# Layer norm's factors and its scale and shift on GpSimd, in a two-layer transformer kernel on one core

## The chip, the cores and the metric

The kernel runs on one NeuronCore of a Trainium2 chip. Five engines work side by side, each through its own instruction queue in program order, and meet at semaphores: TensorE (PE; its weight loads are shown as PEld), VectorE (DVE), ScalarE (ACT), GpSimd (POOL) and SyncE (SP), which here issues the DMAs. The metric is the device time of one execution in microseconds (us).

## The reference

Four residual blocks on x of 16 x 512 x 128 floats (16 batches, 512 tokens, 128 features), each behind a layer norm without learned weights:

```
def _layernorm(x, axis=-1, eps=1e-05):
    m = jnp.mean(x, axis=axis, keepdims=True)
    v = jnp.var(x, axis=axis, keepdims=True)
    return (x - m) / jnp.sqrt(v + eps)
...
x = x + attention0(_layernorm(x))   # 16 heads of 8 features, softmax, output projection and bias
x = x + gated_ffn(_layernorm(x))    # silu(x @ wg.T) * (x @ wu.T) @ wd.T, 384 hidden features
x = x + attention1(_layernorm(x))   # as layer 0, with an rms norm on q and k
x = x + lora_mix(_layernorm(x))     # base linear, plus 8 experts of rank 8 weighted by a softmax router
```

Everything on the way to the change is float32.

## The kernel before

A batch's 512 tokens lie as 4 tiles of 128 partitions. The work is written out by hand as a pipeline over batches of alternating slots, X i and Y i; slots X 2 to Y 13 are one hardware loop of 12 turns, the others are written out. A slot has 32 steps s, each with two half-steps h = 2s and 2s+1, and in a half-step every engine has its fixed share, in program order:

- TensorE: one score tile for the attention (`attend_score`, L1112, banks 0 to 2 of PSUM), one score tile for the running maximum of the next attention (`max_score`, L1102, banks 3 to 5), every fourth half-step the product with the values (`attend_pv`, L1127), and at set half-steps a "piece" of the dense work, all pieces through one PSUM bank (`gen`).
- ScalarE: one exponential for each half-step (`exp_unit`, L647), which frees the attention's bank, and copies of pieces out of PSUM.
- VectorE: one row maximum for each half-step (`max_tile`, L853), which frees the maximum's bank, and the small reductions.
- GpSimd: products that need only SBUF (L539 to L575).

Each of the two score streams has three banks, so TensorE can be three half-steps ahead of the exponential and three ahead of the maximum. Where the maximum's stream passes from one attention to the next (half-steps 38 and 39) the second tile of the new one waits for the last maximum of the old one, two half-steps back (`free_at`, L127).

There are four norms for each batch, told apart by k: norm 1 (before the feed-forward part), norm 2 (before attention 1), norm 3 (before the expert part) and norm 0, which normalises the batch two ahead, straight from `x_in`. Norms 1, 0 and 2 lie in a Y slot, norm 3 in an X slot. A norm goes through the engines like this. VectorE takes statistics (`stats`, L830, `bn`), folds them into mean and variance (`moments`, L838, `mv`) and begins the factors (`factors_in`, L844 and L845: `neg_mean` = -mean, `vpe` = variance + eps, four columns each). GpSimd takes `rstd` = vpe ** -0.5 (L532) and `shift` = neg_mean * rstd (L534). ScalarE applies them, one instruction for each of the four token tiles (`apply_norm`, L653: `xn` = x * rstd + shift). TensorE turns `xn` (`turn_norm`, L1078), and ScalarE copies the result to `xnt`. The places are: norm 1 moments and factors at h 21 of Y, applied at s 12, turned at h 27; norm 0 statistics at h 30 and 32, moments at h 34, factors at h 36, applied at s 21 and 22, turned at h 3 of the next X; norm 2 moments and factors at h 45, applied at s 24, turned at h 51; norm 3 moments at h 27, factors at h 28 of X, applied at s 17 and 18, turned at h 39.

Between norm 1 and norm 2 the feed-forward part runs: `w_gate` product, tanh (`th`, L697), `gs` on VectorE (L902), `w_up` product, `up`, `ht` = up * gs on GpSimd (`up_mul`, L568), three times. The `w_up` product writes the bank that `gs` reads, so it waits for `gs`. `parts_high` and `parts_low` (L859, L868) split finished maxima every sixteenth half-step.

At the start, slot Y -1 works alone: norm 0 of batches 0 and 1, the first projections, the weights.

## Time and profile before

| | |
|---|---|
| runs | 2129.20, 2131.88, 2137.05 us; median 2131.88 |
| profiled execution | 2135.92 us, its span 2134.1 us |
| PE busy | 1831.3 us (86%) |
| DVE busy | 1598.7 us (75%) |
| ACT busy | 1432.2 us (67%) |
| POOL busy | 432.8 us (20%) |

The busy time of an engine says how much lies in its queue, not whether others wait for it; of TensorE it is modelled. What decides are the waits: which instruction stood last before TensorE could go on. The rows for that are below, from slot Y 8 (1086.0 to 1151.0 us of the span), which is one turn of the loop like the others. In a timeline row the first number is the start, the second the time that the group took, and a bracket tells how long the engine stood idle before it and what released it; neighbouring instructions of one engine overlap by up to 0.1 us, so a duration is a little more than the place it takes in the queue.

### The profile page before, as it was taken

The page shows a single profiled execution, that of the slowest core. Times are in us where ns is not written, and L with a number is a line of the kernel's source. Part 1 is how long each engine was busy: PE and PEld are TensorE (multiplying, and loading weights), DVE is VectorE, ACT ScalarE, POOL GpSimd, SP SyncE. Part 2 cuts the span into 40 slices and gives each one's busy share as a digit, 9 for nine tenths or more (in the row PEclk, how much of TensorE's full clock was granted, in tenths as well). Part 3 has the DMA queues.
Part 4 walks back from the last instruction along what each step waited for, and adds up shares of the span by engine and source line. Part 5 has one row for each costly group of instructions (what it writes and reads, how often), then busy time and mean ns, then how long its engine had stood idle before and what let it go on. Part 6 is the DMA issues. An engine that isn't in the chain of part 4 may idle for free.

```text
span 2134.1 us, 38850 instructions
## 1 busy us (share of the span) xinstructions
PE 1831.3 (86%) x10958; PEld 688.9 (32%) x10958; DVE 1598.7 (75%) x3593; ACT 1432.2 (67%) x2921; POOL 432.8 (20%) x570
## 2 busy tenths in 40 slices
PE   4858989888988988888898888989898998998775
PEld 1232323333332333333333333323333332333322
DVE  4538888887878778778787878777787878888471
ACT  2716686776767677677766767676776768776543
POOL 2112131221212122121212212120121213121200
PEclk9957999999999999999999999999999999999867
DMA  5203223050413205041320504123050413212020
GB/s 109 71 11 101 47 67 96 18 140 17 118 34 96 65 17 140 17 115 37 81 81 17 140 17 115 36 71 91 17 140 17 115 37 79 79 35 59 29 53 16
DMA packets 162647, 140.87 MB, mean 66 GB/s; under 512 B 38761, under 2 KB 144050, under 8 KB 162482
## 3 DMA queue, kind: packets, MB, share of 16 engines
q1 hardware_dynamic: 162482, 139.29, 24.7%
q14 instruction: 137, 1.12, 0.2%
q8 instruction: 28, 0.46, 0.1%
HBM read 77.38 MB, written 55.57 MB: 62 GB/s over the span
## 4 chain that ended last, share of the span: by engine, by line
PE 37%; issue 24%; DMA 11%; ACT 9%; POOL 8%; DVE 8%; SPq 3%; ACTq 0%; POOLq 0%; DVEq 0%
PE ps L1127 11%; PE ps L1112 7%; PE ps L1148 5%; ACT probs L647 5%; DVE neg_max L853 4%; PE ps L1102 4%; DMA k_stack<-k_rows 4%; DMA rden_all<-rden_rows 3%; PE ps L1078 3%; PE ps L1153 2%; PE ps L1191 2%; DMA k_rows<-kp 2%; PE ps L1141 2%; POOL o_raw L551 2%; POOL qk L561 2%
## 5 line engine op out<-in xcount | busy, mean ns | idle before, releaser
L853 DVE TENSOR_REDUCE neg_max<-ps 128x1 f32<-128x512 f32 x2048 | 1316.4, 680 | 196.8 <-PE ps L1102 167.7
L647 ACT ACTIVATE probs<-ps 128x512 f32<-128x512 f32 x2048 | 1093.4, 599 | 324.5 <-PE ps L1112 309.0
L1102 PE MATMUL ps<-k_stack,q_stack 48*128 48x512 bf16 x2048 | 702.5, 402 | 86.6 <-DVE neg_max L853 46.4
L1112 PE MATMUL ps<-q_stack,k_stack 50*128 50x512 bf16 x2048 | 655.1, 391 | 79.8 <-ACT probs L647 75.7
L1127 PE MATMUL ps<-probs,v_aug 128*32 128x512 f32 x4096 | 568.1, 628 | 1.0
L1112 PEld LDWEIGHTS ps<-q_stack,k_stack 50*128 50x128 bf16 x2048 | 150.8, 95 | 525.1 <-ACT probs L647 342.4
L1102 PEld LDWEIGHTS ps<-k_stack,q_stack 48*128 48x128 bf16 x2048 | 159.3, 94 | 280.3 <-DVE neg_max L853 239.4
L551 POOL TENSOR_TENSOR o_raw<-o_raw,rden_all 128x512 f32<-128x512 f32 x64 | 81.3, 1270 | 569.6 <-DMA rden_all<-rden_rows 569.6
L1127 PEld LDWEIGHTS ps<-probs,v_aug 128*32 128x32 f32 x4096 | 81.7, 109 | 136.3 <-issue 81.5
L1153 PE MATMUL ps<-wo,o_raw 128*128 128x128 f32 x512 | 81.8, 326 | 43.2 <-POOL o_raw L551 43.1
L653 ACT ACTIVATE xn<-x,shift,rstd 128x128 f32<-128x128 f32 x192 | 80.5, 484 | 52.4 <-POOL shift L534 52.4
L568 POOL TENSOR_TENSOR ht<-up,gs 128x512 f32<-128x512 f32 x48 | 60.9, 1269 | 248.6 <-ACT up L628 248.6
L561 POOL TENSOR_TENSOR qk<-qk,nw_y 128x128 f32<-128x128 f32 x128 | 47.3, 407 | 304.8 <-DVE nw_y L940 304.8
L532 POOL TENSOR_TENSOR rstd<-vpe,half_neg 128x4 f32<-128x4 f32 x64 | 64.5, 1008 | 211.6 <-DVE vpe L845 211.6
L890 DVE TENSOR_TENSOR x<-ps,res 128x512 f32<-128x512 f32 x32 | 22.1, 691 | 105.4 <-PE ps L1153 105.4
L1153 PEld LDWEIGHTS ps<-wo,o_raw 128*128 128x128 f32 x512 | 75.1, 233 | 69.7 <-issue 42.8
L628 ACT ACTIVATE xnt<-ps 128x512 f32<-128x512 f32 x64 | 38.0, 593 | 79.0 <-PE ps L1078 78.6
L1078 PE MATMUL ps<-ident,xn 128*128 128x128 f32 x256 | 57.3, 364 | 31.8 <-ACT xn L653 31.8
L890 DVE TENSOR_TENSOR x<-ps,x 128x512 f32<-128x512 f32 x32 | 22.1, 691 | 83.0 <-PE ps L1191 49.0
L628 ACT ACTIVATE up<-ps 128x512 f32<-128x512 f32 x48 | 28.7, 597 | 63.3 <-PE ps L1148 63.3
L1078 PEld LDWEIGHTS ps<-ident,xn 128*128 128x128 f32 x256 | 36.8, 180 | 97.8 <-issue 97.8
L1148 PE MATMUL ps<-xnt,w_gate 128*128 128x256 f32 x192 | 58.2, 428 | 8.9 <-ACT xnt L628 3.2
(103 smaller groups left out, 1499.4 us busy)
## 6 DMA issues: line engine op xcount, KB each, us to landing
q_stack<-q_rows SPq DMA_DIRECT2D x128, 192.0 KB, 3.7
k_stack<-k_rows SPq DMA_DIRECT2D x128, 192.0 KB, 4.6
rden_all<-rden_rows SPq DMA_DIRECT2D x64, 256.0 KB
q_rows<-qp SPq DMA_DIRECT2D x32, 384.0 KB, 2.6
k_rows<-kp SPq DMA_DIRECT2D x32, 384.0 KB, 2.9
q_rows<-qp SPq DMA_DIRECT2D x32, 256.0 KB, 3.0
k_rows<-kp SPq DMA_DIRECT2D x32, 256.0 KB, 3.0
x_in<-in_L_attn_x SPq DMA_DIRECT2D x16, 256.0 KB, 2.8
```

What stands on the lines that cost most here:

```text
L551: pool.tensor_tensor(o_raw[l][:, c, :], o_raw[l][:, c, :], rden_all[l][:, c, :], ALU.mult).then_inc(att_ready[l], 1)
L561: last = pool.tensor_tensor(x[:, t, :, :], x[:, t, :, :], wide(inv[:, t, :, None], 2, HD), ALU.mult)
L628: return act.activation(dst, src, ACT.Copy)
L647: act.activation(probs[:, u % RING, :], ps[:, bank_of(l, u), :], ACT.Exp).then_inc(exps, 1)
L653: last = act.activation(xn[k][:, t, :], x[:, t, :], ACT.Identity, bias=shift[k][:, t:t + 1], scale=rstd[k][:, t:t + 1])
L853: dve.tensor_reduce(neg_max[l][:, pair // 2, col:col + 1], ps[:, BANKS + bank_of(l, n), :], AX.X, ALU.max, negate=True).then_inc(max_taken, 1)
L1078: return pe.transpose(dst, src, ident[0:n, 0:n])
L1102: pe.matmul(ps[:, BANKS + bank_of(l, m), :], q_stack[l][row:row + KROWS, pair, tok:tok + 128], k_stack[l][row:row + KROWS, pair, :], start ...
L1112: pe.matmul(ps[:, bank_of(l, u), :], k_stack[l][row:row + AROWS, pair, tok:tok + 128], q_stack[l][row:row + AROWS, pair, :], start=True, s ...
L1127: last = pe.matmul(acc[32 * j:32 * j + 32, :], v_aug[l][:, kt, 8 * e + 2 * group + pp, :], probs[:, (u + j) % RING, :], start=(s == 0 and ...
L1148: return pe.matmul(gen[:, 256 * half:256 * half + 256], w, xt[:, 256 * half:256 * half + 256], start=True, stop=True)
L1153: last = pe.matmul(gen4[:, t, :], o_raw[l][:, c, 128 * t:128 * t + 128], wo[l][:, c, :], start=c == 0, stop=c == 1)
```

## The change

`neg_mean` and `factors_in` go. GpSimd computes `vpe` itself and the shift from the mean with its sign kept, and it applies the norm, four instructions of 128 x 128 with two operands read per partition (x * rstd - shift). ScalarE's `apply_norm` goes, with all its calls.

```diff
             def norm_factors(k, b):
+                wait_apart(pool, mv_done[k], b + 1, passed)
+                pool.tensor_scalar(vpe[k][:, :], mv[k][:, :, 1], LN_EPS, None, ALU.add).then_inc(var_ready[k], 1)
                 pool.wait_ge(var_ready[k], b + 1)
                 pool.tensor_tensor(rstd[k][:, :], vpe[k][:, :], half_neg[:, :], ALU.pow).then_inc(rstd_ready[k], 1)
                 pool.wait_ge(rstd_ready[k], b + 1)
-                pool.tensor_tensor(shift[k][:, :], neg_mean[k][:, :], rstd[k][:, :], ALU.mult).then_inc(shift_ready[k], 1)
+                pool.tensor_tensor(shift[k][:, :], mv[k][:, :, 0], rstd[k][:, :], ALU.mult).then_inc(shift_ready[k], 1)
+            def apply_norm(k, x, b):
+                if k in (0, 3):
+                    need(pool, read[f"xt{k}"], b)
+                elif k == 1:
+                    need(pool, read["xt2"], b)
+                else:
+                    pool.wait_ge(read["xt1"], b + 1)
+                wait_apart(pool, shift_ready[k], b + 1, passed)
+                for t in range(TT):
+                    last = pool.tensor_scalar(xn[k][:, t, :], x[:, t, :], rstd[k][:, t:t + 1], shift[k][:, t:t + 1],
+                                              ALU.mult, ALU.subtract)
+                last.then_inc(xn_ready[k], 1)
...
                     if "M1" in have:
                         normalise(0, 1, i)
                         norm_factors(1, i)
+                        apply_norm(1, x1, i)
                         for c in range(NH):
                             up_mul(c, i)
                     if "S0" in have and at >= 0:
                         norm_factors(0, i + 2)
+                        apply_norm(0, x_in, i + 2)
                     if "M1" in have:
                         norm_factors(2, i)
+                        apply_norm(2, x2, i)
...
-            def apply_norm(k, x, tiles, b):
-                act.wait_ge(shift_ready[k], b + 1)
-                for t in tiles:
-                    last = act.activation(xn[k][:, t, :], x[:, t, :], ACT.Identity, bias=shift[k][:, t:t + 1],
-                                          scale=rstd[k][:, t:t + 1])
-                if tiles[-1] == TT - 1:
-                    last.then_inc(xn_ready[k], 1)
...
-            def factors_in(k, b):
-                dve.wait_ge(mv_done[k], b + 1)
-                dve.tensor_scalar(neg_mean[k][:, :], mv[k][:, :, 0], -1.0, None, ALU.mult)
-                dve.tensor_scalar(vpe[k][:, :], mv[k][:, :, 1], LN_EPS, None, ALU.add).then_inc(var_ready[k], 1)
```

VectorE's order around norm 0 in a Y slot (`gs` is the feed-forward gate, `ht` is on GpSimd). Before:

```order
L838 BN_AGGR mv<-bn 128x2 x4
L853 TENSOR_REDUCE neg_max<-ps 128x1 x2
L844 TENSOR_SCALAR neg_mean<-mv 128x4
L845 TENSOR_SCALAR vpe<-mv 128x4
L853 TENSOR_REDUCE neg_max<-ps 128x1
L859 CAST neg_high<-neg_max 128x16
L902 SCALAR_TENSOR_TENSOR gs<-th,ps 128x512
```

Now:

```order
L840 BN_AGGR mv<-bn 128x2 x4
L848 TENSOR_REDUCE neg_max<-ps 128x1 x3
L854 CAST neg_high<-neg_max 128x16
L897 SCALAR_TENSOR_TENSOR gs<-th,ps 128x512
```

The two small instructions between the second and the third row maximum are gone; nothing else on VectorE moved.

GpSimd's order through norms 1, 0 and 2 of a Y slot. Before:

```order
L532 TENSOR_TENSOR rstd<-vpe,half_neg 128x4
L534 TENSOR_TENSOR shift<-neg_mean,rstd 128x4
L568 TENSOR_TENSOR ht<-up,gs 128x512 x3
L532 TENSOR_TENSOR rstd<-vpe,half_neg 128x4
L534 TENSOR_TENSOR shift<-neg_mean,rstd 128x4
L532 TENSOR_TENSOR rstd<-vpe,half_neg 128x4
L534 TENSOR_TENSOR shift<-neg_mean,rstd 128x4
```

Now:

```order
L531 TENSOR_SCALAR vpe<-mv 128x4
L533 TENSOR_TENSOR rstd<-vpe,half_neg 128x4
L535 TENSOR_TENSOR shift<-mv,rstd 128x4
L547 TENSOR_SCALAR xn<-x,rstd,shift 128x128 x4
L583 TENSOR_TENSOR ht<-up,gs 128x512 x3
L531 TENSOR_SCALAR vpe<-mv 128x4
L533 TENSOR_TENSOR rstd<-vpe,half_neg 128x4
L535 TENSOR_TENSOR shift<-mv,rstd 128x4
L547 TENSOR_SCALAR xn<-x_in,rstd,shift 128x128 x4
L531 TENSOR_SCALAR vpe<-mv 128x4
L533 TENSOR_TENSOR rstd<-vpe,half_neg 128x4
L535 TENSOR_TENSOR shift<-mv,rstd 128x4
```

Behind each shift stand the four instructions that apply the norm, and ahead of each power stands `vpe`; the order of the norms and of `ht` is as it was.

ScalarE's order at the very start (the table load belongs to the first activation). Before:

```order
L653 ACT_TABLE_LOAD
L653 ACTIVATE xn<-x_in,shift,rstd 128x128 x4
L628 ACTIVATE xnt<-ps 128x512
```

Now:

```order
L649 ACT_TABLE_LOAD
L649 ACTIVATE xnt<-ps 128x512
```

The table load, which waited for the shift, now stands behind the wait for the turned tile.

## Rows read from the trace of the kernel before

**Rows 1.** Slots X 8 and X 9: busy us (instructions) of PE, PEld, DVE, ACT, POOL; clock; DMA.
```profile
1027.60:1086.00 58.40, 51.29 (x336) 19.09 (x336) 47.14 (x106) 44.33 (x91) 15.53 (x23) 0.97 0.42 111
...
1151.00:1211.90 60.90, 53.77 (x336) 19.66 (x336) 47.10 (x106) 44.37 (x90) 15.53 (x23) 0.92 0.38 106
```
**Rows 2.** Timeline of VectorE around norm 1 in slot Y 8.
```profile
1107.48 0.38 DVE L838 BATCH_NORM_AGGREGATE mv<-bn 128x2 f32<-128x6 f32 x4
1107.90 0.17 DVE L844 TENSOR_SCALAR neg_mean<-mv 128x4 f32<-128x4 f32 x1
...
1108.05 0.69 DVE L853 TENSOR_REDUCE neg_max<-ps 128x1 f32<-128x512 f32 x1
1108.65 0.17 DVE L868 TENSOR_TENSOR neg_max<-neg_max,neg_high 128x16 f32<-128x16 f32 x1
```
**Rows 3.** Timeline of GpSimd, the same norm.
```profile
1108.22 1.01 POOL L532 TENSOR_TENSOR rstd<-vpe,half_neg 128x4 f32<-128x4 f32 x1 [7.39 <-DVE vpe L845]
1109.30 0.20 POOL L534 TENSOR_TENSOR shift<-neg_mean,rstd 128x4 f32<-128x4 f32 x1
```
**Rows 4.** Timeline of ScalarE, the same norm.
```profile
1109.60 1.63 ACT L653 ACTIVATE xn<-x,shift,rstd 128x128 f32<-128x128 f32 x4
```
**Rows 5.** Timeline of TensorE, the same norm.
```profile
1108.79 0.39 PE L1102 MATMUL ps<-k_stack,q_stack 48*128 48x512 bf16 x1 [0.81 <-DVE neg_max L853]
...
1110.38 1.06 PE L1127 MATMUL ps<-probs,v_aug 128*32 128x512 f32 x8
1111.38 0.66 PE L1078 MATMUL ps<-ident,xn 128*128 128x128 f32 x4
```
**Rows 6.** Timeline of VectorE around norm 0's factors in slot Y 8.
```profile
1121.32 0.69 DVE L853 TENSOR_REDUCE neg_max<-ps 128x1 f32<-128x512 f32 x1 [0.17 <-PE ps L1102]
1121.92 1.07 DVE L844 TENSOR_SCALAR neg_mean<-mv 128x4 f32<-128x4 f32 x1
...
1122.98 0.68 DVE L853 TENSOR_REDUCE neg_max<-ps 128x1 f32<-128x512 f32 x1
1123.69 0.18 DVE L859 CAST neg_high<-neg_max 128x16 bf16<-128x16 f32 x1
1123.87 0.69 DVE L902 SCALAR_TENSOR_TENSOR gs<-th,ps 128x512 f32<-128x512 f32 x1
```
**Rows 7.** Timeline of GpSimd at the same place.
```profile
1121.70 1.26 POOL L568 TENSOR_TENSOR ht<-up,gs 128x512 f32<-128x512 f32 x1 [3.15 <-ACT up L628]
```
**Rows 8.** Timeline of ScalarE at the same place.
```profile
1122.89 0.63 ACT L697 ACTIVATE th<-ps 128x512 f32<-128x512 f32 x1
```
**Rows 9.** Timeline of TensorE at the same place.
```profile
1122.91 0.38 PE L1112 MATMUL ps<-q_stack,k_stack 50*128 50x512 bf16 x1
1123.71 0.39 PE L1102 MATMUL ps<-k_stack,q_stack 48*128 48x512 bf16 x1 [0.43 <-DVE neg_max L853]
1124.03 1.06 PE L1127 MATMUL ps<-probs,v_aug 128*32 128x512 f32 x8
1125.03 1.13 PE L1148 MATMUL ps<-xnt,w_up 128*128 128x256 f32 x4
```
**Rows 10.** Group of all `neg_mean`: busy us, mean ns, idle before.
```profile
L844 DVE TENSOR_SCALAR neg_mean<-mv 128x4 f32<-128x4 f32 x64 | 22.4, 350 | 1.3
```
**Rows 11.** Norm 2 of slot Y 8, timeline of ScalarE.
```profile
1136.40 1.65 ACT L653 ACTIVATE xn<-x,shift,rstd 128x128 f32<-128x128 f32 x4 [0.37 <-POOL shift L534]
```
**Rows 12.** Norm 2 of slot Y 8, timeline of TensorE.
```profile
1138.36 0.66 PE L1078 MATMUL ps<-ident,xn 128*128 128x128 f32 x4
```
**Rows 13.** TensorE in slot X 8, behind the application of norm 3.
```profile
1064.03 0.50 PE L1102 MATMUL ps<-k_stack,q_stack 48*128 48x512 bf16 x2 [1.72 <-DMA k_stack<-k_rows]
```
**Rows 14.** GpSimd's nearest instruction in size, timeline of slot X 8.
```profile
1039.45 2.96 POOL L561 TENSOR_TENSOR qk<-qk,nw_y 128x128 f32<-128x128 f32 x8 [20.31 <-DVE nw_y L940]
```
**Rows 15.** Timeline of ScalarE at the start.
```profile
7.04 1.28 ACT L653 ACT_TABLE_LOAD   x1 [7.04 <-POOL shift L534]
17.30 1.65 ACT L653 ACTIVATE xn<-x_in,shift,rstd 128x128 f32<-128x128 f32 x4 [8.97 <-DVE bq_scaled L983]
```

More of the change, by code:

```diff
@@ L202, in build @@
         rstd = [sb(f"rstd{k}", [128, TT]) for k in range(4)]
-        neg_mean = [sb(f"neg_mean{k}", [128, TT]) for k in range(4)]
         shift = [sb(f"shift{k}", [128, TT]) for k in range(4)]
@@ L598, in slot @@
                         norm_factors(3, i - 2)
+                        apply_norm(3, x3, i - 2)
                         mix(i - 2)
@@ L604, in slot @@
                         norm_factors(0, 0)
+                        apply_norm(0, x_in, 0)
                         for n in (0, 1):
@@ L609, in slot @@
                         norm_factors(0, 1)
+                        apply_norm(0, x_in, 1)
                     if "M1" in have:
@@ L721, in slot @@
                     act.wait_ge(bq_ready, 1)
-                    apply_norm(0, x_in, range(TT), 0)
                     take("xt0", xnt[0][:, :], 0)
@@ L728, in slot @@
                     weights_out()
-                    apply_norm(0, x_in, range(TT), 1)
                     take_max(0, 0, 0)
@@ L764, in slot @@
                         if "E" in have:
-                            if s in (17, 18):
-                                apply_norm(3, x3, (2 * s - 34, 2 * s - 33), i - 2)
                             if s == 19:
@@ L773, in slot @@
                     else:
-                        if "S0" in have and s in (21, 22):
-                            apply_norm(0, x_in, (2 * s - 42, 2 * s - 41), i + 2)
                         if "M1" in have:
-                            if s == 12:
-                                apply_norm(1, x1, range(TT), i)
                             if s == 13:
@@ L784, in slot @@
                                 take_up((s - 15) // 2, i)
-                            if s == 24:
-                                apply_norm(2, x2, range(TT), i)
                             if s == 25:
@@ L980, in slot @@
                     moments(0, 0)
-                    factors_in(0, 0)
                     dve.wait_ge(first_loaded, 16 * 6)
@@ L990, in slot @@
                     moments(0, 1)
-                    factors_in(0, 1)
                 for h in range(2 * STEPS):
@@ L1019, in slot @@
                                 moments(3, i - 2)
-                            if h == 28:
-                                factors_in(3, i - 2)
                             if h in (43, 44, 45):
@@ L1035, in slot @@
                                 moments(0, i + 2)
-                            if h == 36:
-                                factors_in(0, i + 2)
                         if "V0" in have and h in (16, 17):
@@ L1051, in slot @@
                                 moments(1, i)
-                                factors_in(1, i)
                             if at == 0 and h == 23:
@@ L1063, in slot @@
                                 moments(2, i)
-                                factors_in(2, i)
                             if h in (53, 55):
```

## The prediction

> **What bounds the kernel now.** I read the busy times first, then the waits, then timelines of one turn of the loop around each norm. No engine is full: in slot X 8, of 58.40 us, TensorE is busy 51.29, VectorE 47.14, ScalarE 44.33, GpSimd 15.53 [rows 1]. TensorE goes in program order through both score streams and stops where either ring of three banks is not free, so what counts at each norm is which engine frees the bank that TensorE asks for next. At norm 1 that is VectorE: TensorE idled 0.81 us for a row maximum just after the moments [rows 5], and VectorE goes through its maxima there without a gap. At norm 0's factors it is VectorE again (0.43 us idle, and a start 0.80 us after the score tile ahead of it, 1123.71 against 1122.91) [rows 9]. Behind norm 3 it is neither: TensorE waits 1.72 us for a DMA that fills the next key stack [rows 13].
>
> ScalarE's part is 4 instructions in 1.63 us at norm 1 [rows 4]. The exponentials behind them are late by that, but TensorE is meanwhile in the value product (1110.38 to 1111.38) and then in the turn (1111.38 on) [rows 5]; it asks for none of these exponentials before it is through. So the time that ScalarE loses is mostly not on the path, and the 16 x 4 x 1.65 = 106 us that it gets back are no term of my sum.
>
> **The two instructions that go from VectorE.** Without a neighbour on GpSimd they are short: the moments end at 1107.48 + 0.38 = 1107.86, the next maximum starts at 1108.05 [rows 2], so they take 0.19 us of VectorE's queue.
>
> At norm 0 it is another thing: `neg_mean`, four columns, takes 1.07 us [rows 6]. It starts at 1121.92, while GpSimd's `ht` runs from 1121.70 to 1122.96, and ends just behind it [rows 7]. In all, `neg_mean` is busy 22.4 us [rows 10]; 64 at 0.17 make 10.9, and the other 11.5 at 0.90 each make 13 such cases: norm 0 of batches 3 to 15, one in each turn in which `ht` runs beside it. The Trainium skill (SBUF — State Buffer, "Who interferes with whom") has this as an exclusive lock that VectorE's two-port or two-input instructions share with GpSimd; the trace agrees.
>
> What is the stall worth? Without the two instructions the maximum at 1122.98 starts at 1121.92, 1.06 earlier. The score tile that waits for it (1123.71) can follow its predecessor at 1122.91, 0.80 earlier, so the value product goes from 1124.03 to 1123.23 and the `w_up` product from 1125.03 to 1124.23 [rows 9]. But that product also needs `gs`, and `gs` needs the tanh, which ends at 1122.89 + 0.63 = 1123.52 [rows 8]; `gs` then runs from 1123.55 for 0.69 and frees the bank about 0.05 later, at 1124.29. `gs` is what is late next, and the place gives 1125.03 - 1124.30 = 0.73 us. The cast (L859), in front of `gs`, would wait for `ht` in its turn, until 1122.96, which is 0.4 us before `gs` can start: covered by the tanh. Behind that TensorE and ScalarE take turns on the feed-forward's pieces, all of which move together. **13 x 0.73 = 9.5 us.**
>
> **The chain from moments to the turn.** Now, at norm 1: moments end 1107.86, power 1108.22 to 1109.23, shift 1109.30 to 1109.50, application 1109.60 to 1111.23, turn 1111.38 [rows 2 to 5]: 3.52 us. TensorE comes out of a value product 1.00 us after its start (1124.03 to 1125.03 in [rows 9]), here at 1110.38 + 1.00 = 1111.38 too: chain and queue end together.
>
> After: a handover (0.09, as `vpe` ended 1108.13 and the power began 1108.22), `vpe` on GpSimd (0.20, the price of its shift, four columns too), handover 0.08, power 1.01, handover 0.08, shift 0.20, handover 0.08, three starts and one full application, 0.14 to TensorE. That is 1.88 + 3t + d, with t from start to start of an application and d the length of the last. No row shows the application's form on GpSimd (128 columns, one tensor, two scalars per partition). Its bound from below is the 0.20 of the shift [rows 3]; the nearest row is `scale_qk`, two tensors of 128 columns: 8 in 2.96 us, that is a start every t = 0.36 and d = 0.41 for one alone [rows 14]; from above it is the power's 1.01 [rows 3]. I take the nearest, since it has the same columns: 1.88 + 1.09 + 0.41 = 3.38 us, 0.14 less than now.
>
> The Trainium skill (GPSIMD Engine Reference, 3.1) gives one-input bodies 1.03 cycles for each element and two-input ones about 2.6; an estimate by it is 128 x 1.03 / 1.2 GHz = 0.11 us and the fixed 0.2, some 0.3 us an instruction in place of 0.36 to 0.41. By that the chain is 0.3 us shorter still, and norm 1's gain below goes from 0.14 to its limit of 0.19, 0.8 us in all.
>
> At norm 1 VectorE's 0.19 brings TensorE to the turn 3.33 us after the moments, xn comes at 3.38: the gain is 0.14. **16 x 0.14 = 2.2 us.** At norm 2, application ends 1138.05 [rows 11], turn 1138.36 [rows 12]; the chain is 0.17 us ahead of TensorE, which comes through VectorE's maxima as before. Both gain, so VectorE's 0.19 counts in full. **16 x 0.19 = 3.0 us.** At norm 3 what VectorE gives up is swallowed by the 1.72 us of DMA wait [rows 13], whose chain began earlier: 0. Norm 0's application is turned a slot later: 0. GpSimd's longer queue (0.2 + 1.5 us for each norm) delays nobody at these places: it stood idle 7.39 us ahead of norm 1's power [rows 3], and 3.15 us ahead of the second `ht` [rows 7].
>
> **The start.** Now ScalarE waits until 17.30 (a late load of the first projections' biases), applies for 1.65, and TensorE follows 0.14 later; the table load was over by then [rows 15]. After, GpSimd has xn long before, and TensorE turns as soon as the loads are in; but the table load (1.28) now stands behind the wait for that turn. Gain 1.65 + 0.14 - 1.28 = **0.5 us**; the first slots and the last norm have the bare chain, 3 x 0.14 = **0.4 us**.
>
> Sum: 9.5 + 2.2 + 3.0 + 0.5 + 0.4 = 15.6 us. Against the profiled execution that is 2135.9 - 15.6 = 2120.3 us; the median of the runs lies 4.0 below that execution: **2116.3 us**, 0.73% faster. A difference under 0.5% (10.7 us) is about what a measurement of this kernel can't tell from none.
>
> **The clock.** X 8 took 58.40 us at a granted clock of 0.97, X 9 60.90 at 0.92, with the same work [rows 1]. So the dips to the lower level (1.2 in place of 2.4 GHz), which come in short stretches behind pauses of TensorE, move single slots by up to 2.5 us. 0.8 us of pause goes in each turn, others shift; I put +-7 us on the sum for it and leave the middle.
>
> **Rivals.** (a) GpSimd's application is slow. The chain is 1.88 + 4t + 0.05 and each 0.1 us on t costs 0.4 us at 32 turns. It eats the other 10 us when 16(1.93 + 4t - 3.52) + 16(1.93 + 4t - 3.64) = 10, at t = 0.49, and makes the kernel slower by over 0.5% from t = 0.58. For it: two scalars are read per partition, which no GpSimd row has, and the power takes 1.01 us for four columns. At t = 0.75 it is 43 - 10 = +33 us: 2165 us. Against it: it is a plain multiply and subtract with one tensor. Chance 0.16, of which 0.04 ends within 0.5%.
>
> (b) The lock moves. GpSimd is busy 1.7 us longer for each norm; a VectorE instruction that needs the shared pair and comes in that stretch waits, by up to 0.9 us as above. Perfetto Trace Analysis of the Trainium skill ("Optimizing Scalar/DVE Operations") says for this that offloading between the two might not help. Behind norm 1 stands L868, which reads two SBUF tensors; it took 0.17 us at 1108.65 while the power ran [rows 2, 3], and is over before the application; at the others I find maxima out of PSUM. If one instruction a turn loses 0.7 us all the same, 16 x 0.7 = 11 us go back: 2127 us. The same time comes if the 0.73 is absorbed by the next wait. Chance 0.20.
>
> (c) ScalarE's relief pays. If TensorE did lack the late exponentials, norms 1 and 2 would give half of 1.63 us more each: 32 x 0.8 = 26 us, 2090 us. [rows 4, 5] speak against it. Chance 0.12.
>
> My forecast has 0.52; within it the clock leaves about 0.09 inside 0.5%. **Faster by over 0.5%: 0.43 + 0.12 = 0.55; within: 0.09 + 0.20 + 0.04 = 0.33; slower: 0.12.** Range: the forecast with the clock and t from 0.25 to 0.45 spans 2107 to 2128, (b) takes it to 2134; to leave no more than 0.2 out I reach some way to (c) and (a): 2100 to 2138 us.
>
> **What would show it.** No VectorE instruction of about 1 us beside `ht`; `w_up` of the third gate 0.7 us sooner behind its tanh; GpSimd's four applications in 1.5 us; moments to turn 3.4 us at norm 1 and TensorE waiting for xn by 0.05 us; ScalarE's busy time 106 us less with more idle time in front of its exponentials; the same DMA wait behind norm 3. I am wrong if t is over 0.45, if L859 or L868 stretch, or if slots X shrink as much as slots Y.

## The result, and the profile after

The changed kernel takes 2238.68 us (median of 4 runs, 2232.58 to 2243.99), the kernel before 2132.68 us beside it: a ratio of 1.0495, 95% interval 1.0461 to 1.0529. It is 4.95% slower, 106 us; the forecast was 2116.3 us with 2138 as its upper end. The profiled execution of the changed kernel has a span of 2242.2 us, that of before 2134.1.

First the page of the changed kernel: ScalarE's busy time fell from 1432.2 us to 1339.5, by 93 us (the forecast had 106), and GpSimd's rose from 432.8 to 650.4, by 218 us.

```profile
PE 1885.5 (84%) x10958; PEld 693.6 (31%) x10958; DVE 1583.6 (71%) x3465; ACT 1339.5 (60%) x2665; POOL 650.4 (29%) x890
...
PEclk8858999899898988999899899988999999998867
```

The groups of GpSimd's new instructions, in the view by line (busy us, mean ns of one, idle time before it): the applications, 192 for norms 1 to 3 and 64 for norm 0, then the power, `vpe` and the shift, which cost about what was supposed.

```profile
L547 POOL TENSOR_SCALAR xn<-x,rstd,shift 128x128 f32<-128x128 f32 x192 | 150.4, 796 | 9.6 <-issue 7.2 <-POOL shift L535 2.2
L547 POOL TENSOR_SCALAR xn<-x_in,rstd,shift 128x128 f32<-128x128 f32 x64 | 50.0, 795 | 3.0 <-issue 2.4 <-POOL shift L535 0.5
L533 POOL TENSOR_TENSOR rstd<-vpe,half_neg 128x4 f32<-128x4 f32 x64 | 66.4, 1037 | 5.3
L531 POOL TENSOR_SCALAR vpe<-mv 128x4 f32<-128x4 f32 x64 | 15.0, 234 | 142.3 <-DVE mv L840 142.1
L535 POOL TENSOR_TENSOR shift<-mv,rstd 128x4 f32<-128x4 f32 x64 | 12.9, 202 | 5.0
```

An application takes 0.80 us. The same norm 1 of slot Y 8 as in [rows 2 to 5], now in the timelines of VectorE, GpSimd and TensorE:

```profile
1161.58 0.38 DVE L840 BATCH_NORM_AGGREGATE mv<-bn 128x2 f32<-128x6 f32 x4
1161.88 0.66 DVE L848 TENSOR_REDUCE neg_max<-ps 128x1 f32<-128x512 f32 x1
```

```profile
1162.16 0.23 POOL L531 TENSOR_SCALAR vpe<-mv 128x4 f32<-128x4 f32 x1 [5.61 <-DVE mv L840]
1162.48 1.04 POOL L533 TENSOR_TENSOR rstd<-vpe,half_neg 128x4 f32<-128x4 f32 x1
1163.60 0.20 POOL L535 TENSOR_TENSOR shift<-mv,rstd 128x4 f32<-128x4 f32 x1
1164.00 3.13 POOL L547 TENSOR_SCALAR xn<-x,rstd,shift 128x128 f32<-128x128 f32 x4 [0.20 <-issue]
```

```profile
1162.60 0.39 PE L1089 MATMUL ps<-k_stack,q_stack 48*128 48x512 bf16 x1 [0.51 <-DVE neg_max L848]
...
1164.19 1.07 PE L1114 MATMUL ps<-probs,v_aug 128*32 128x512 f32 x8
1167.27 0.75 PE L1065 MATMUL ps<-ident,xn 128*128 128x128 f32 x4 [2.01 <-POOL xn L547]
```

The moments end at 1161.58 + 0.38 = 1161.96, xn is there at 1164.00 + 3.13 = 1167.13, the turn starts at 1167.27: 5.31 us behind the moments where it was 3.52. Four applications in 3.13 us, 0.80 for the last, are a start every (3.13 - 0.80) / 3 = 0.78 us. TensorE is through with its value product at 1165.26 and stands for 2.01 us. Norm 2 is the same, with a turn at 5.30 us behind the moments where it was 3.64:

```profile
1196.41 0.63 PE L1065 MATMUL ps<-ident,xn 128*128 128x128 f32 x4 [1.88 <-POOL xn L547]
```

After the change both numbers are the same in nearly every turn of the loop. Before, norm 1 had 3.52 in most turns and up to 4.3 in some, and norm 2 had 4.5 or 4.6 in five.

TensorE's waits for xn in all (us, times, longest), after:

```profile
PE ps L1065 <- POOL xn L547: 76.0, 33, 7.3
```

Before, it waited at 5 places, the longest of them 19.1 us at the start:

```profile
PE ps L1078 <- ACT xn L653: 31.8, 5, 19.1
```

At the place of [rows 6 to 9], in the next stretch of slot Y 8, now ScalarE and TensorE, and VectorE beside GpSimd's `ht`:

```profile
1180.00 0.63 ACT L709 ACTIVATE th<-ps 128x512 f32<-128x512 f32 x1
```

```profile
1181.41 0.48 PE L1135 MATMUL ps<-xnt,w_up 128*128 128x256 f32 x1
```

```profile
1178.43 1.29 DVE L848 TENSOR_REDUCE neg_max<-ps 128x1 f32<-128x512 f32 x2 [0.17 <-PE ps L1089]
1179.76 0.37 DVE L854 CAST neg_high<-neg_max 128x16 bf16<-128x16 f32 x1
1180.67 0.69 DVE L897 SCALAR_TENSOR_TENSOR gs<-th,ps 128x512 f32<-128x512 f32 x1 [0.54 <-ACT th L709]
```

```profile
1178.83 1.27 POOL L583 TENSOR_TENSOR ht<-up,gs 128x512 f32<-128x512 f32 x1 [3.14 <-ACT up L649]
```

No instruction of 1.07 us is left here; the cast waits for the end of `ht` (0.37 us, it was 0.18) and is over 0.5 us before the tanh ends. The `w_up` product starts 1181.41 - 1180.63 = 0.78 us behind the tanh, where it was 1125.03 - 1123.52 = 1.51: the 0.73 us of the forecast, to the hundredth. It is so in every turn: at the third gate the distance was 1.51 at 13 places and 0.78 at 3, and is 0.77 or 0.78 at all 16.

A third thing changed, TensorE's clock. In the stretch from 300 to 1900 us the granted clock was 0.96 before and is 0.92 after (the second row below is after's, the first before's; behind the times come the busy times of PE, PEld, DVE, ACT and POOL, then the clock):

```profile
300.00:1900.00 1600.00, 1428.64 (x8831) 534.79 (x8828) 1278.93 (x2869) 1147.10 (x2346) 343.44 (x445) 0.96 0.26 70
```

```profile
300.00:1900.00 1600.00, 1400.06 (x8406) 513.31 (x8398) 1208.28 (x2645) 1026.65 (x2045) 501.88 (x684) 0.92 0.25 67
1080.00:1141.80 61.80, 54.31 (x340) 19.76 (x339) 47.93 (x106) 43.09 (x87) 18.96 (x28) 0.92 0.41 104
1209.30:1274.70 65.40, 58.13 (x339) 20.54 (x338) 48.08 (x106) 43.08 (x86) 18.95 (x28) 0.84 0.38 99
```

The last two rows are the changed kernel's slots X 8 and X 9, with the same work. The records of the clock in these traces have two values, full and half, so a granted clock of 0.92 is (1 - 0.92) x 2 x 61.80 = 9.9 us at the lower, and 0.84 is 20.9 us: 11.0 us more at the lower clock made the slot 3.6 us longer, **about 0.33 us for each us**. The line through X 3 to X 13 of this kernel, length against time at the lower clock, has a slope of 0.34. In all runs the mean clock was 0.930 for before (65 runs beside the experiments) and 0.899 for after (4): 299 and 452 us at the lower level.

Where the added stretches begin can be seen in the trace. In the two rows below the first is the norm 1 above up to the turn, the second the 3.4 us behind the wait for xn:

```profile
1160.00:1167.60 7.60, 5.07 (x30) 1.42 (x30) 5.58 (x18) 3.59 (x8) 4.60 (x7) 1.00 0.12 36
1167.60:1171.00 3.40, 3.40 (x13) 1.44 (x13) 1.29 (x2) 1.68 (x3) 0.00 (x0) 0.51 0.00 0
```

From 300 to 1900 us the changed kernel waits 24 times for 1.9 to 2.0 us for xn, and at 19 of these places a stretch at the lower clock begins, from 0.4 us ahead of the wait's end to 2.1 us behind it. They are 19 of its 45 such stretches and 68 us of its 249 at the lower clock. Before had 126 us there, in 32 stretches, and no wait for xn of this length. Another 72 us, in 10 stretches, begin behind the wait for the DMA of the key stack in slot X, where before had 17 us in 5; why these grew the traces don't show.

### The profile page after: what moved, and what is told of

Read it like the earlier page. It is cut to its first block and busy times, and to the rows that moved or that the text cites. A ratio compares the mean times of both kernels' runs of the same rounds, so it can differ in the third digit from the quotient of the medians.

```text
span 2242.2 us, 38884 instructions
## 1 busy us (share of the span) xinstructions
PE 1885.5 (84%) x10958; PEld 693.6 (31%) x10958; DVE 1583.6 (71%) x3465; ACT 1339.5 (60%) x2665; POOL 650.4 (29%) x890
## 5 line engine op out<-in xcount | busy, mean ns | idle before, releaser
L1089 PE MATMUL ps<-k_stack,q_stack 48*128 48x512 bf16 x2048 | 727.0, 418 | 91.7 <-DVE neg_max L848 46.5
L1099 PE MATMUL ps<-q_stack,k_stack 50*128 50x512 bf16 x2048 | 683.1, 408 | 64.9 <-ACT probs L668 60.5
L1114 PE MATMUL ps<-probs,v_aug 128*32 128x512 f32 x4096 | 586.4, 647 | 0.9
L566 POOL TENSOR_TENSOR o_raw<-o_raw,rden_all 128x512 f32<-128x512 f32 x64 | 81.2, 1268 | 517.3 <-DMA rden_all<-rden_rows 517.3
L547 POOL TENSOR_SCALAR xn<-x,rstd,shift 128x128 f32<-128x128 f32 x192 | 150.4, 796 | 9.6 <-issue 7.2
L1140 PE MATMUL ps<-wo,o_raw 128*128 128x128 f32 x512 | 71.9, 299 | 46.5 <-POOL o_raw L566 46.5
L1140 PEld LDWEIGHTS ps<-wo,o_raw 128*128 128x128 f32 x512 | 65.6, 208 | 73.0 <-issue 44.6
L1135 PE MATMUL ps<-xnt,w_gate 128*128 128x256 f32 x192 | 69.2, 495 | 7.5 <-ACT xnt L649 1.5
L590 POOL TENSOR_TENSOR coef<-gating,rm 128x64 f32<-128x64 bf16 x64 | 16.7, 292 | 197.1 <-DVE gating L963 197.1
L897 DVE SCALAR_TENSOR_TENSOR gs<-th,ps 128x512 f32<-128x512 f32 x48 | 33.0, 688 | 57.1 <-ACT th L709 57.1
```

The lines of the kernel that those rows point to most:

```text
L547: last = pool.tensor_scalar(xn[k][:, t, :], x[:, t, :], rstd[k][:, t:t + 1], shift[k][:, t:t + 1], ALU.mult, ALU.subtract)
L566: pool.tensor_tensor(o_raw[l][:, c, :], o_raw[l][:, c, :], rden_all[l][:, c, :], ALU.mult).then_inc(att_ready[l], 1)
L1089: pe.matmul(ps[:, BANKS + bank_of(l, m), :], q_stack[l][row:row + KROWS, pair, tok:tok + 128], k_stack[l][row:row + KROWS, pair, :], start ...
L1099: pe.matmul(ps[:, bank_of(l, u), :], k_stack[l][row:row + AROWS, pair, tok:tok + 128], q_stack[l][row:row + AROWS, pair, :], start=True, s ...
L1114: last = pe.matmul(acc[32 * j:32 * j + 32, :], v_aug[l][:, kt, 8 * e + 2 * group + pp, :], probs[:, (u + j) % RING, :], start=(s == 0 and ...
L1135: return pe.matmul(gen[:, 256 * half:256 * half + 256], w, xt[:, 256 * half:256 * half + 256], start=True, stop=True)
```

## The experiments

Each kernel's change against before is given by its ratio x 2136 us. "Chain" is the time from the end of the moments to the turn at norm 1 and norm 2, read in slot Y 8 as above.

**1. The application alone.** Before, with the four applications on GpSimd; the factors stay begun on VectorE. Since VectorE still negates the mean, the shift is added.

```diff
+            def apply_norm(k, x, b):
+...
+                    last = pool.tensor_scalar(xn[k][:, t, :], x[:, t, :], rstd[k][:, t:t + 1], shift[k][:, t:t + 1],
+                                              ALU.mult, ALU.add)
```

> The kernel before with the application alone moved to GpSimd; VectorE still begins the factors. Theory A (GpSimd's application takes 0.78 us from start to start, the chain from moments to turn grows from 3.5 to about 5.1 us at norms 1 and 2, and TensorE's longer pauses there bring more stretches at the lower clock): about +100 us, 2225 to 2245, granted clock near 0.90, neg_mean still 1.07 us at norm 0. Rival B (the loss comes from the factors on GpSimd, or from GpSimd and VectorE together): well under +60 us.

2130.59 us, ratio 0.9979 (0.9949 to 1.001): the time is where rival B had it, and theory A, which I held for nearly certain, that this half carries the slowness, missed by about 95 us. It fell with this row, the group of the applications:

```profile
L545 POOL TENSOR_SCALAR xn<-x,rstd,shift 128x128 f32<-128x128 f32 x192 | 83.8, 453 | 9.3 <-issue 7.2 <-POOL shift L534 1.9
```

0.453 us and not 0.796, a start every 0.43 us; chain 3.74 and 3.74 us. The same engine, shape and operands; the only thing that differs is the second operation, add in place of subtract. ScalarE is relieved of as much as in the changed kernel (1338.0 us busy), and nothing comes of it: rival (c) is out.

**2. The factors alone.** Before, with `vpe` and `neg_mean` computed on GpSimd; ScalarE applies.

```diff
+                wait_apart(pool, mv_done[k], b + 1, passed)
+                pool.tensor_scalar(vpe[k][:, :], mv[k][:, :, 1], LN_EPS, None, ALU.add)
+                pool.tensor_scalar(neg_mean[k][:, :], mv[k][:, :, 0], -1.0, None, ALU.mult).then_inc(var_ready[k], 1)
```

> The kernel before with the factors alone moved to GpSimd (one more small instruction there, the negated mean); ScalarE applies. Theory A: the 1.07 us of VectorE beside ht goes (about -9 us), the chain grows by 0.2 to 0.3 us at norms 1 and 2 (about +8 us): 2124 to 2138, clock 0.93. Rival B: clearly slower than before, 2170 or more.

2131.83 us, ratio 0.9977 (0.9946 to 1.0007). Chain 3.98 and 3.95 us, since a second short instruction stands ahead of the power; what the stall gives back goes into that. The time is in theory A's range for this half, and rival B, that the factors carry the loss, is out. So neither half, as these two kernels have it, makes the kernel slow; but the first had an add where the changed kernel has a subtract.

**3. Work in TensorE's wait.** The changed kernel, with 8 matmuls of zeros (bf16, 512 columns) ahead of the wait for xn at norms 1 and 2.

```diff
+                if k in (1, 2):
+                    fill(FILL)
                 pe.wait_ge(xn_ready[k], b + 1)
```

> The changed kernel with 8 matmuls of zeros (bf16, 512 columns, some 1.7 us at the full clock) on TensorE ahead of its wait for xn at norms 1 and 2, into the PSUM bank that the turn then overwrites. The wait is the same length, TensorE is busy in it. Theory A (half of the loss is the clock that falls behind the pause): 2175 to 2195 us, granted clock back to 0.93 or more, chain still 5.3 us. Rival C (all of the loss is waits; the clock's dips cost little): 2235 or more, since work is only added.

2209.1 us, ratio 1.0339 (1.0305 to 1.0373): between the two. The mean clock came back to 0.930 with a chain of 5.22 and 5.21 us, but the run has a cost of its own. In the waits of TensorE (us in total, times, longest) and in the DMA queues of this kernel:

```profile
PE ps L1102 <- issue: 59.5, 22, 3.3
...
q8 instruction: 128, 2.10, 0.4%
```

59.5 us in which TensorE waited for nothing that the profile shows, at 22 places at the loop's turn, and 128 packets of instructions in place of 28. I read this as TensorE fetching instructions anew in each turn of the longer program. The Trainium skill (Runtime: NRT & Kernel Launch, "Instruction fetch mechanics") has a stall of this kind for a taken branch whose target is not in the fetched window; the trace agrees, with 2.7 us each.

**4. Norm 0's factors early.** Before, with the two VectorE instructions of norm 0 issued right behind its moments, ahead of `ht`, and nothing else.

```diff
                                 moments(0, i + 2)
-                            if h == 36:
                                 factors_in(0, i + 2)
```

> The kernel before with norm 0's two factor instructions put right behind its moments (half-step 34 instead of 36), ahead of GpSimd's ht. Theory A of the stall (0.73 us a turn is on TensorE's path): neg_mean 0.17 us everywhere, 2118 to 2127 us. Rival D (what follows absorbs it): 2130 to 2134.

2124.74 us, ratio 0.9932 (0.9909 to 0.9955), 14.5 us faster. The group of `neg_mean`, 22.4 us in [rows 10]:

```profile
L844 DVE TENSOR_SCALAR neg_mean<-mv 128x4 f32<-128x4 f32 x64 | 10.7, 167 | 1.7
```

The distance from tanh to `w_up` is 0.78 us at all 16 places here too. **The stall's term of my sum (9.5 us) is confirmed by itself**, if anything too small (the interval is 9.6 to 19.4 us), and its cure needs two lines moved, and no other engine.

**5. One word.** The changed kernel with add in place of subtract. It computes something else (the mean is added and not taken away); the work is the same.

```diff
-                                              ALU.mult, ALU.subtract)
+                                              ALU.mult, ALU.add)
```

> The changed kernel with one word altered: the second operation of the application on GpSimd is an add in place of the subtract. What it computes is changed by that, the mean is added and not taken away; the work is otherwise the same. Theory (the subtract is what costs): an application starts every 0.43 us as in the run with the application alone, in place of 0.78, the chain from moments to turn at norm 1 is 2.04 + 3 x 0.43 + 0.45 + 0.14 = 3.9 us; against before that is +0.4 us at 16 turns of norm 1 and +0.25 at 16 of norm 2, and -9.5 (the stall beside ht) -6 (two short instructions gone from VectorE): 2125 to 2134 us. Rival (the move as a whole costs, by GpSimd's queue or by VectorE's casts beside it, and the word does little): 2200 us or more, with an application every 0.78 us still, or every 0.43 and the time kept.

2127.18 us, ratio 0.9941 (0.9912 to 0.9971), by the ratios 118 us below the changed kernel. The group of the applications, and GpSimd at norm 1 of slot Y 8:

```profile
L547 POOL TENSOR_SCALAR xn<-x,rstd,shift 128x128 f32<-128x128 f32 x192 | 83.3, 448 | 9.6 <-issue 7.2 <-POOL shift L535 2.2
...
1097.87 1.74 POOL L547 TENSOR_SCALAR xn<-x,rstd,shift 128x128 f32<-128x128 f32 x4 [0.20 <-issue]
```

Chain 3.92 and 3.91 us. VectorE is as busy as in the changed kernel (1582.7 us against 1583.6). **The whole loss hangs on the subtract.**

**6. Prices of forms.** Before, with instructions on tiles of their own at GpSimd's start.

```diff
+            pool.tensor_scalar(f1[:, 0:128], t_in[:, 0:128], t_s[:, 0:1], t_s[:, 1:2], ALU.mult, ALU.subtract)
+...
```

> Before, with some 35 instructions on tiles of their own put into GpSimd's start, to price forms of 128 and 512 float32 columns. Theory A (subtract itself is slow on GpSimd when its operand is a per-partition value): mult+add with two per-partition operands 0.43 us, mult+subtract 0.78, subtract alone with one such operand slower than mult alone by 0.35, subtract of two tensors as mult of two tensors (0.36). Theory B (only mult+add is a fused case and every other pair runs in two passes): subtract+mult and add+mult 0.78 too, and subtract alone as mult alone. With 512 columns the gap is 4 times as wide if it is a cost for each element, and the same 0.35 if it is a fixed one. The time of the whole is a few us over before.

One execution, 2143.07 us, made for its rows and not for its time. One row of each form from GpSimd's timeline. In this order: multiply and add; multiply and subtract; subtract and multiply; add and multiply; the first two with 512 columns (L557, L558); one scalar per partition, multiply (L559) and subtract (L562); two constants, multiply and add (L566), multiply and subtract (L569); two tensors, subtract (L572) and multiply (L575).

```profile
2.62 0.44 POOL L546 TENSOR_SCALAR f<-t_in,t_s 128x128 f32<-128x128 f32 x1
4.25 0.79 POOL L549 TENSOR_SCALAR f<-t_in,t_s 128x128 f32<-128x128 f32 x1
6.59 0.79 POOL L552 TENSOR_SCALAR f<-t_in,t_s 128x128 f32<-128x128 f32 x1
8.57 0.45 POOL L555 TENSOR_SCALAR f<-t_in,t_s 128x128 f32<-128x128 f32 x1
9.42 0.77 POOL L557 TENSOR_SCALAR f<-t_in,t_s 128x512 f32<-128x512 f32 x1
10.17 2.08 POOL L558 TENSOR_SCALAR f<-t_in,t_s 128x512 f32<-128x512 f32 x1
12.23 0.60 POOL L559 TENSOR_SCALAR f<-t_in,t_s 128x128 f32<-128x128 f32 x1
13.97 0.61 POOL L562 TENSOR_SCALAR f<-t_in,t_s 128x128 f32<-128x128 f32 x1
15.97 0.30 POOL L566 TENSOR_SCALAR f<-t_in 128x128 f32<-128x128 f32 x1
17.12 0.64 POOL L569 TENSOR_SCALAR f<-t_in 128x128 f32<-128x128 f32 x1
18.75 0.45 POOL L572 TENSOR_TENSOR f<-t_in 128x128 f32<-128x128 f32 x1
19.98 0.45 POOL L575 TENSOR_TENSOR f<-t_in 128x128 f32<-128x128 f32 x1
```

With two operations a subtract makes the instruction 0.35 us longer, in either place and with constants too (0.30 against 0.64). It is a price for each column: from 128 to 512 columns multiply and add grow by 0.33 us, 0.86 ns a column, multiply and subtract by 1.29 us, 3.36 ns a column. Two tensors cost 0.45 whether subtracted or multiplied, and with one operation and one scalar subtract and multiply are alike. So theory A was half right (it expected the single subtract to be slow) and theory B fell (add and multiply is as fast as multiply and add). A single operation with a scalar per partition takes 0.60, more than the two operations multiply and add; I can't say why.

**7. Two fillers in place of eight.** As 3, with two float32 matmuls, to keep the program short.

```diff
+                if k in (1, 2):
+                    pe.matmul(gen, filler[:, 0:128], filler[:, :], start=True, stop=True)
+                    pe.matmul(gen[:, 0:256], filler[:, 0:128], filler[:, 0:256], start=True, stop=True)
```

> The changed kernel with two float32 matmuls of zeros (512 and 256 columns, about 1.5 us together) on TensorE ahead of its wait for xn at norms 1 and 2; they are two instructions in place of the eight of the run before, so that TensorE's instruction stream is hardly longer. Theory (the long wait costs twice: 1.7 us direct at each of 32 turns, about 55 us, and the stretches at the lower clock behind it, the rest of the +106 with the stall's 9.5 and VectorE's 6 given back: about 60): no instruction waits of 2.6 us at the loop back, low stretches back to about the 126 us of before in the loop, and 2242 - 60 = 2165 to 2190 us. Rival (the clock is a bystander and the direct wait makes all of it): 2230 us or more with the clock at 0.93.

2185.33 us, ratio 1.0225 (1.0178 to 1.0271). The time is in the range expected, one sign is not: the fetch is there again, once a turn and longer.

```profile
PE ps L1101 <- issue: 47.9, 11, 4.6
...
1177.97 0.60 PE L1101 MATMUL ps<-q_stack,k_stack 50*128 50x512 bf16 x1 [4.44 <-issue]
```

Still the chain is as long as in the changed kernel (5.22 and 5.21 us), instruction fetches of 47.9 us come on top, and by the ratios it is 58 us faster than the changed kernel, with a mean clock of 0.938 against 0.899. So the rival is out (the direct wait does not make all of it), and the busy waits are worth at least these 58 us (45 to 70 by the two intervals). How much the clock makes can't be read from this run, since part of the fetch's 47.9 us is hidden.

**8. The application shared.** As 2, and at norms 1 and 2 ScalarE applies tiles 0 and 1, GpSimd tiles 2 and 3, with multiply and add.

```diff
+            def apply_half(k, x, b):
+...
+                for t in (2, 3):
+                    last = pool.tensor_scalar(xn[k][:, t, :], x[:, t, :], rstd[k][:, t:t + 1], shift[k][:, t:t + 1],
+                                              ALU.mult, ALU.add)
+...
-                                apply_norm(1, x1, range(TT), i)
+                                apply_norm(1, x1, (0, 1), i)
```

> Before, with both factors computed by GpSimd (as in the run of factors alone), and the application of norms 1 and 2 shared: ScalarE tiles 0 and 1, GpSimd tiles 2 and 3 with mult and add and the negated shift. Norms 0 and 3 are applied by ScalarE. Theory (my sum holds once the chain is no longer than before): chain 2.3 to the shift's end + 0.1 + 2 x 0.43 + 0.14 = 3.35 us, so 9.5 us for the stall and 16 x 2 x 0.17 = 5.5 for VectorE's queue come through: 2132 - 15 = 2117, 2112 to 2122 us. Rival (what VectorE gives up at norms 1 and 2 is not on the path): as the early norm 0, 2122 to 2127. Rival (the shared application costs in another way, xn in two halves or GpSimd beside VectorE's casts): 2130 or more.

**2102.92 us, ratio 0.9852 (0.9805 to 0.9899): the fastest kernel of the study**, 31.6 us below before, twice what its terms gave and outside of every range expected. The chain is 3.40 and 3.37 us. Norm 1 in slot Y 8, GpSimd, ScalarE, TensorE:

```profile
1091.35 0.89 POOL L546 TENSOR_SCALAR xn<-x,rstd,shift 128x128 f32<-128x128 f32 x2 [0.21 <-issue]
```

```profile
1091.18 0.88 ACT L669 ACTIVATE xn<-x,shift,rstd 128x128 f32<-128x128 f32 x2 [0.65 <-POOL shift L537]
```

```profile
1092.39 0.63 PE L1079 MATMUL ps<-ident,xn 128*128 128x128 f32 x4
```

**9. The same move with the right form.** All on GpSimd as in the change, but as (x + negated mean) x rstd, without a shift.

```diff
+                pool.tensor_scalar(shift[k][:, :], mv[k][:, :, 0], -1.0, None, ALU.mult).then_inc(var_ready[k], 1)
...
+                    last = pool.tensor_scalar(xn[k][:, t, :], x[:, t, :], shift[k][:, t:t + 1], rstd[k][:, t:t + 1],
+                                              ALU.add, ALU.mult)
```

> The changed kernel's move, all of it on GpSimd and with the right result, but written as (x + the negated mean) x rstd: add, then multiply. GpSimd computes vpe and the negated mean, then the power; there is no shift. Theory (the subtract alone made the change slow): 0.43 us from start to start, chain 0.20 + 0.25 + 0.1 + 1.01 + 0.2 + 3 x 0.43 + 0.45 + 0.14 = 3.65 to 3.95 us, as the run with the add in place of the subtract: 2118 to 2132 us. Rival (with the right values, or with the add first, it is slow): 2200 us or more.

2123.3 us, ratio 0.9949 (0.9922 to 0.9977), chain 3.97 and 3.96 us. What the change does, written so, is 0.5% faster than before; it is no better than moving two lines (4).

**10. Norm 0 early, and the application shared.** VectorE keeps its two instructions at norms 1 and 2.

```diff
                                 moments(0, i + 2)
-                            if h == 36:
                                 factors_in(0, i + 2)
...
                         norm_factors(1, i)
+                        apply_half(1, x1, i)
...
-                                apply_norm(1, x1, range(TT), i)
+                                apply_norm(1, x1, (0, 1), i)
```

> Before, with norm 0's factors begun on VectorE right behind its moments (as in the run of that alone) and the application of norms 1 and 2 shared between ScalarE (tiles 0, 1) and GpSimd (tiles 2, 3, multiply and add). VectorE keeps both of its short instructions. It asks what made the shared kernel 31 us faster where its terms gave 15. Theory A (what VectorE gives up at norms 1 and 2, 0.30 us each, is on the path once the chain is short): here TensorE comes out of its value product 3.5 us behind the moments as before, the chain of 2.7 us is ahead of it and gives nothing: 2118 to 2126 us, as with norm 0's factors early alone. Theory B (slack in the chain spares pauses and with them stretches of the lower clock): fewer of them, 15 to 20 in the loop in place of 30, and 2100 to 2112 us.

2125.12 us, ratio 0.9946 (0.9921 to 0.997): theory A. GpSimd's half of the application ends early, and the turn stands where it stood:

```profile
1109.33 0.88 POOL L543 TENSOR_SCALAR xn<-x,rstd,shift 128x128 f32<-128x128 f32 x2 [0.20 <-issue]
```

```profile
1110.01 1.06 PE L1139 MATMUL ps<-probs,v_aug 128*32 128x512 f32 x8
1111.00 0.66 PE L1090 MATMUL ps<-ident,xn 128*128 128x128 f32 x4
```

xn is ready at 1110.21, and TensorE turns at 1111.00, 3.52 us behind the moments as before, since it comes out of its value product only then. A shorter chain is worth nothing without VectorE's 0.3 us, and those are worth nothing without a short chain (2). Only both together (8) gain.

**11 and 12. One norm slow.** Kernel 9, with the changed kernel's own lines (subtract, 0.78 us a tile) for norm 1 alone, and for norm 2 alone.

```diff
-                        norm_factors(1, i)
-                        apply_norm(1, x1, i)
+                        norm_factors_sub(1, i)
+                        apply_norm_sub(1, x1, i)
```

> The kernel with add and multiply on GpSimd for norms 0, 2 and 3, and the changed kernel's own lines (multiply and subtract, 0.78 us a tile) for norm 1 alone: half of the slow applications on the path. The chain at norm 1 is 1.4 us longer than with the add. Theory (each long wait costs twice, direct and by the clock behind it): 16 x 1.4 = 22 us direct and about as much by lower clock, 2160 to 2185 us. Rival (the clock's share came from both waits lying in one slot, or from norm 3): the direct part alone, 2140 to 2150 us.

2169.85 us, ratio 1.017 (1.0132 to 1.0208).

> The counterpart of the run before: add and multiply for norms 0, 1 and 3, the changed kernel's own lines (0.78 us a tile) for norm 2 alone. Direct cost over the kernel with add and multiply everywhere: 16 x 1.4 = 22 us. With norm 1 slow the profile showed no more time at the lower clock than with none slow (113 us in the loop), with both slow 249. Theory P (it is the wait at norm 2, the last before slot X, that brings the lower clock): over 200 us low in the loop and 2175 to 2195 us. Theory C (only both together do, since the second long wait comes when the first has hardly been made good): about 110 to 150 us low and 2150 to 2170 us.

2183.78 us, ratio 1.0241 (1.018 to 1.0302). Over kernel 9 the one costs 47 us, the other 62 (to within 10 and 14 us), together 109; the changed kernel lies 117 above kernel 9 (1.0495 - 0.9949). So the times add up, and theory C, that only both together bring the loss, is out. Theory P was right in time and only partly in its sign: from 300 to 1900 us the profiled run has 184 us at the lower clock, not over 200. The same stretch has 113 us in kernel 9, 113 with norm 1 slow and 249 in the changed kernel. With norm 1 slow, 9 of the 13 long waits there have a lower stretch right behind them, but the profiled run has no more of it in all.

## What makes the 106 us

The experiments give an account with two terms: **direct**, 16 x what the chain grew at norm 1 (from 3.52) + 16 x the same at norm 2 (from 3.64) - 9.5 us where the stall is gone; and **clock**, 0.34 us for each us more at the lower clock than before ran beside it (mean of all runs; the changed kernel against the 282 us of before's profiled run; against the mean of the 65 runs it would be +153 and the sum +98). For kernel 10 at norm 2 the table has the 3.64 us of most turns; slot Y 8 had 4.04.

| kernel | chain, norm 1 / 2 | direct | lower clock, more than before | sum | measured |
|---|---|---|---|---|---|
| changed | 5.31 / 5.30 | +45.7 | +170 | +103 | +106 ±7 |
| 1 application alone | 3.74 / 3.74 | +5.1 | -10 | +2 | -4 ±7 |
| 2 factors alone | 3.98 / 3.95 | +2.8 | -16 | -3 | -5 ±7 |
| 4 norm 0 early | 3.52 / 3.64 | -9.5 | -19 | -16 | -15 ±5 |
| 5 one word | 3.92 / 3.91 | +1.2 | -32 | -10 | -13 ±6 |
| 8 shared | 3.40 / 3.37 | -15.7 | -51 | -33 | -32 ±10 |
| 9 add, multiply | 3.97 / 3.96 | +2.8 | -22 | -5 | -11 ±6 |
| 10 early and shared | 3.52 / 3.64 | -9.5 | -14 | -14 | -12 ±5 |
| 11 norm 1 slow | 5.32 / 3.95 | +24.3 | +16 | +30 | +36 ±8 |
| 12 norm 2 slow | 3.96 / 5.31 | +24.3 | +68 | +47 | +51 ±13 |
| 3 eight fillers | 5.22 / 5.21 | +42.8 | +9 | +46 | +72 ±7 |
| 7 two fillers | 5.22 / 5.21 | +42.8 | -34 | +31 | +48 ±10 |

Ten rows agree within about their intervals. The two with fillers miss by 26 and 17 us, which is the part of their 59.5 and 47.9 us of instruction waits that nothing hides. So of the changed kernel's 106 us, about 55 are the longer waits of TensorE for xn, -9.5 the stall, and some 58 the clock behind these waits. The split is no better than this: by the mean over the turns, in place of slot Y 8, the longer waits are 47 us and not 55. The clock's price is a slope over slots that differ in more than the clock, and over the 65 runs of before, span against time at the lower clock, the slope is 0.22 and not 0.34, which would leave 37 us of the 58 and 23 of the loss unexplained. What needs no such price is kernel 7, whose filled waits gave back 58 us.

That the waits cause the lower clock is shown by the stretches that begin right behind them, by the filled waits of 3 and 7, and by kernels 11 and 12: against kernel 9 (22 us less than before) norm 1's wait alone brings 38 us of it, norm 2's 90, and both together 192 (means of 4 to 10 runs, which scatter by 20 to 35 us a run). Why a wait at norm 2 brings more than one at norm 1 stays open.

## Why the prediction was wrong

- **The price of the application (t) is the step that failed.** I took 0.36 us from `scale_qk` [rows 14], "since it has the same columns"; it is 0.78. The columns and even the operand kinds were not what decides, the operation is: with add it would have been 0.43 and the time within the forecast's range, as kernel 9 (2123.3 us) shows. The 2.2 and 3.0 us that I gave norms 1 and 2 would have failed even so: kernel 9's chain is 3.97 us where I had 3.38. No row of before had a subtract beside another operation. My reason against rival (a), "a plain multiply and subtract with one tensor", named the very thing that made it slow.
- **Rival (a) had the mechanism and nearly the price** (t = 0.75). Its break-even of 0.49 is too high: the chain measured is 2.19 + 4t (5.31 at 0.78, 3.92 at 0.43), by which the same sum comes out even at 0.42. Kernels 5 and 9, at 0.43, have a direct part of +1 and +3 us; that they are 13 and 11 us faster than before goes with less time at the lower clock. And (a) gave 2165 us. With the gains taken off, its waits made 33 us where the account has 45.7: `vpe` starts 0.20 us behind the moments and not 0.09, takes 0.23 and not 0.20, and the application starts 0.20 behind the shift and not 0.08, so the chain is 5.31 and not 1.93 + 4 x 0.78 = 5.05. And (a) had no term for the clock, which I had put at ±7 us "for shifts" and which made some 58. A wait of 2 us in place of 0.1 is no shift; that is what put 2238 outside of every case that I had.
- **The range** (2138 at its upper end) left nearly all of rival (a) out on the strength of a chance of 0.16 that rested on this one row. With the chain and the clock priced as the experiments price them, (a) would have been 2132 + 103 = 2235.
- **The stall: right.** 0.73 us at 13 places, to be seen by itself in kernel 4 and at the `w_up` product after; the covering tanh held, and the cast took the wait on as described.
- **VectorE's two instructions: right in kind, too small.** I took 0.19 us, the gap between moments and next maximum. After the change, that maximum starts 0.08 ahead of the moments' end (1161.88 against 1161.96), so the difference is 0.27; TensorE's value product starts 1164.19 - 1161.96 = 2.23 us behind the moments with both its parts, against 1110.38 - 1107.86 = 2.52 before: 0.29 us earlier. In the changed kernel this came to nothing at both norms, for the chain was by far the later of the two.
- **Rival (b), the lock moves: seen, and worth nothing.** The casts rose from 183 to 238 ns in the mean, 7 us in all, beside `ht` and under the tanh.
- **Rival (c), ScalarE's relief pays: no.** Kernel 1 relieves it as much and gains at most 11 us by its interval, of 26, or 16 with the 5 us that its longer chain costs.
- **Norm 3: right**, xn still comes ahead of the DMA. **The start: right in kind.** The table load (1.28 us) stands behind the turn's wait, and the first copy starts at 19.68 in place of 20.21: 0.5 us.

```profile
18.39 1.28 ACT L649 ACT_TABLE_LOAD   x1 [18.39 <-PE ps L1065]
19.68 0.60 ACT L649 ACTIVATE xnt<-ps 128x512 f32<-128x512 f32 x1
```

## What to carry to other kernels

When an instruction goes to another engine, price its own form there, operations and operand kinds together; if no row shows it, take the break-even seriously and put the chance by how far the nearest row is in *every* respect, not in size alone. A cost on TensorE's path is to be priced with the clock behind it: here a wait grown from 0.1 to 2 us cost about twice its length. Where chain and queue end together, neither alone can be shortened with profit; and an instruction that stalls beside another engine's may need only another place in its own queue.

## What I had not expected of the hardware

- On GpSimd an instruction with two operations takes 0.79 us at 128 columns if one is a subtract, 0.44 with multiply and add; 2.08 against 0.77 at 512. With two tensors, subtract costs as much as multiply (0.45). The Trainium skill (GPSIMD Engine Reference, 3.1) has 1.03 cycles for each element at 1.2 GHz for one input, 0.86 ns; the trace agrees for multiply and add (0.86 ns a column) and not with a subtract in it (3.36 ns, 4.0 such cycles).
- Four or sixteen more matmuls in each turn of TensorE's loop (two or eight at each of two norms) made it wait for instructions at each turn, 4.4 us once or 2.7 us twice, with 127 or 128 packets of instructions in place of 28. An instruction that is added to a long loop body can have a price of its own that its duration doesn't show.
- A wait of 1.9 to 2.0 us was followed within about 2 us by a stretch at the lower clock at 19 of 24 places, and eight bf16 or two float32 matmuls of zeros in the wait brought the mean clock from 0.899 back to 0.930 and 0.938.
- Over 65 runs of the kernel before, the span lay between 2115.7 us (granted clock 0.946) and 2148.6 us (0.917), with a correlation of -0.80 between clock and span: most of this kernel's scatter goes with the clock.
